# Gate factors held with channels on partitions and applied after y is turned back, with ScalarE sharing the taking out of y

## The chip, the cores and the metric

The kernel runs on one core of one Trainium2 chip. The metric is the time of one execution on the device in microseconds (us); lower is better. The engines of the core are named as in the profile: PE is TensorE, DVE is VectorE, ACT is ScalarE, POOL is GpSimd, SP is SyncE, which issues the transfers.

## The reference

Four layers stand one behind the other, on x of shape (2, 1024, 256). Layers 0 and 3 are attention layers, which the change leaves alone. Layer 1 is a Mamba block and layer 2 a block with two state-space scans, one forward and one backward. Cut to what matters, with 512 channels and 16 states:

```python
# layer 1, both batches
xm, z = split(h @ W_in)                  # 512 channels each
xm = silu(causal_conv(xm) + conv_b)
y = scan(xm) + xm * D_param              # hst = hst * dA + dt*x*B ; y = sum over states of hst * C
out = (y * silu(z)) @ W_out              # z is the gate factor, one for each token and channel

# layer 2, both batches
u1, u2 = two projections of the normed tokens xs
y = scan_forward(u1) + u1 * Dp1 + scan_backward(u2) + u2 * Dp2
out = (y * silu(xs @ Wx.T + bx)) @ Wf.T + bf
```

## The kernel before

Every scan is a *run*: run 0 and run 1 are layer 1 on batch 0 and 1, runs 2 and 3 are the forward and backward scan of layer 2 on batch 0, runs 4 and 5 the same on batch 1. In the code `r.q` is the run's number and `r.n` its kind: 0 for layer 1, 1 for a forward scan of layer 2, 2 for a backward one. A run goes over two halves of 512 tokens (`r.order`, the first is p=0 and the second p=1), and within a half over 16 states and 4 blocks of 128 channels: 128 units, which are handled in 64 pairs. The work of one pair passes through the engines like this:

- PE forms u for each unit into one of the PSUM banks 4 to 7 (`form_u`: L757 or L762), and ACT makes the decay factors (`decay`, L844) and the scaled inputs (L821, L828).
- DVE runs the recurrence along the tokens (L897, one instruction for a unit).
- POOL multiplies a pair with C (L912, one instruction for a pair).
- PE turns the product so that tokens are on partitions and adds it up in PSUM banks 0 to 3 (`add_up`, L781, eight transposes for a pair). Bank j holds y for 128 tokens and all 512 channels.

Between DVE and PE there are five pair buffers (`HS`), so DVE can be at most five pairs ahead of `add_up`. Every engine does its instructions in the order in which the code writes them; engines wait for each other through counters (`wait_ge`).

y is taken out of banks 0 to 3 twice in a run: at unit 71 (`TAKEN_AT`) for the first half, and at the end for the second. DVE does it, one instruction for a bank: in layer 1 it multiplies by silu(z) while taking out (`gated`, L1093), in run 2 and 4 it copies (L1212), in run 3 and 5 it multiplies by the gate factor MX (L1215). Runs 3 and 5 first add what runs 2 and 4 left, through an identity matmul into the same banks (`add_before`, L792).

Behind runs 0, 1, 3 and 5 comes what this text calls the *tail*: `turn_back_t` turns y so that channels are on partitions again, with 32 transposes into eight banks (L920), ACT copies them out (`turn_back_s`, L927), and PE multiplies by W_out or Wf (`tokens_t`, L265). Meanwhile DVE goes on with what stands next in its own order: behind run 1 `norm2_v` for batch 0 and behind run 3 `norm2_v` for batch 1 (two normalisations, one behind the other, L206 to L217, with L973 and L975 between them, and each with one instruction of POOL, L230). Behind run 5 it is `norm3_v` for batch 0 (one normalisation). Then follow the instructions that take the projection out of PSUM: L1101 behind runs 0 and 1, and L1227, L1230, L1232 behind runs 3 and 5. The next layer's first transposes on PE (L243) and its first projection (L256) read what `norm2_v` made.

Ahead of runs 3 and 5, `inputs_t` prepares the run, and `gates_t` computes the gate factors of layer 2 there: for each of eight token tiles a bias matmul (L195) and two matmuls (L1145). ACT applies silu (`gates_s`, L1152). The last four of these have to wait until the last gate is computed, since they overwrite what the gates read (XS):

```python
        XS = area(2048, 2, S)
        MX = area(2048, TB, E)
```

Of the kernel before, what the change touches and what calls it, by code (L numbers as in the profile page):

```python
# [111 lines left out]
def program(nc, T, out):  # L112
    with ExitStack() as ctx:
# [626 lines left out]
        def run_t(e, w, r, before=None):  # L740
# [24 lines left out]
            def open_y(ci, j):  # L765
# [4 lines left out]
                if ci == r.order[0]:  # L770
                    w.wait_ge(*(dve if j < 2 else act).at(("dut", q, 1, j)))
                else:
                    w.wait_ge(*taken.at((q, r.order[0], j)))
# [34 lines left out]
            banks.at, banks.held = 4, [[("last y", q, j)] for j in range(4)] + [[("last u", q, j)] for j in range(4)]  # L808

        def run_s(e, w, r, meanwhile=None):  # L810
# [51 lines left out]
            for i in range(UNITS):  # L862
                k, dt = divmod(i, 4)
                if i >= 4:
                    decay(i)
# [4 lines left out]
                else:  # L870
                    spread_b(i // 8 * 2 + 3, i // 2 % 4)

        TAKEN_AT = 71

        def run_v(e, w, r, take_out):
            q = r.q

            def take_y(ci, pair):
                w.wait_ge(*added.at((q, pair)))
                for j in range(4):  # L880
                    take_out(e, w, 4 * ci + j, PS[:, j, :], (q, ci, j))
# [32 lines left out]
        def turn_back_t(e, w, key, src, ready):  # L914
            for c in range(2):
                for m in range(4):
                    o = take(w, (key, c, m))
                    ready()
                    for j in range(4):
                        t = e.transpose(o[:, j * 128:(j + 1) * 128], src[:, 4 * c + j, m * 128:(m + 1) * 128], ident[:, :])  # L920
                    t.then_inc(*pe.up((key, c, m)))

        def turn_back_s(e, w, key, dst):
            for c in range(2):
# [890 lines left out]
```

## Time and profile before

| what | value |
| --- | --- |
| median of 3 runs | 2087.67 us (2085.17 to 2089.85) |
| time of the profiled execution | 2090.79 us |
| its span in the profile | 2089.0 us |
| busy share: PE, DVE, ACT, POOL | 93%, 76%, 69%, 50% |
| granted clock of PE, mean over the span | 0.969 |

The span is what the profiler saw of the core; the device time of that execution is 1.79 us longer. The busy shares are means over all four layers. POOL stands idle in the first and the last layer and works almost without a break in the six runs, so what bounds a stage must be read from that stage. The granted clock is 1.00 at 2.4 GHz and 0.50 at 1.2 GHz.

### The profile page before, as it was taken

To read this page: it belongs to the slowest core of one execution; us is meant where nothing else is said; L and a number is where in the kernel's file an instruction comes from. 1 tells how busy PE (TensorE), PEld (TensorE's weight loads), DVE (VectorE), ACT (ScalarE), POOL (GpSimd) and SP (SyncE) were. 2 spreads that over 40 slices of the span, in tenths; PEclk is the share of its full clock that TensorE was granted. 3 is DMA by queue.
4 is the path that set the end of the run, shared out by engine and by line. 5 is a ranking of instruction groups with operands and counts; after the bars stand their busy time and mean duration, and the time that the engine had idled before them with its cause. 6 is when DMAs were issued, how large, how long until landed. Compare 5 with 4: busy or idle time off the path is not lost.

```text
span 2089.0 us, 32428 instructions
## 1 busy us (share of the span) xinstructions
PE 1939.5 (93%) x12376; PEld 1356.1 (65%) x12376; DVE 1585.7 (76%) x2084; ACT 1436.9 (69%) x2434; POOL 1035.9 (50%) x598
## 2 busy tenths in 40 slices
PE   6989999899999899989998999899988999999997
PEld 3754999659985799589965998599853222222222
DVE  5556899469984899689974998699859777777632
ACT  3426998389964999598827996898642566655664
POOL 3021799209981599379930997299724000002000
PEclk9989999999999999999999999999999999999999
DMA  5031211111111111011100111111101111111000
GB/s 188 1 129 43 72 56 57 41 39 57 57 41 52 39 58 57 22 36 57 52 10 12 57 57 42 40 53 56 36 16 40 33 33 32 33 33 32 9 21 21
DMA packets 57369, 95.04 MB, mean 45 GB/s; under 512 B 14903, under 2 KB 23383, under 8 KB 55806
## 3 DMA queue, kind: packets, MB, share of 16 engines
q1 hardware_dynamic: 55678, 88.77, 14.1%
q0 software_dynamic: 1536, 4.20, 0.7%
q8 instruction: 98, 1.61, 0.3%
q14 instruction: 57, 0.47, 0.1%
HBM read 73.42 MB, written 6.91 MB: 38 GB/s over the span
## 4 chain that ended last, share of the span: by engine, by line
PE 72%; DVE 10%; issue 6%; POOL 6%; ACT 4%; DMA 1%; SPq 0%; POOLq 0%; DVEq 0%; ACTq 0%
PE PS L757 14%; PE PS L781 12%; PE PS L762 7%; PE PS L256 7%; PE PS L1409 5%; DVE A L1422 5%; PE PS L1457 5%; POOL A L912 5%; PE PS L265 4%; PE PS L1602 3%; PE PS L788 2%; PE PS L1145 1%; PE PS L441 1%; PE PS L644 1%; PE PS L1036 1%
## 5 line engine op out<-in xcount | busy, mean ns | idle before, releaser
L912 POOL TENSOR_TENSOR A<-A 128x1024 f32<-128x1024 f32 x384 | 898.4, 2387 | 333.7 <-ACT small L836 265.9
L844 ACT ACTIVATE A<-A,negA 128x512 f32<-128x512 f32 x768 | 545.0, 712 | 42.5 <-DVE A L897 32.9
L897 DVE TENSOR_TENSOR_SCAN A<-A,PS 128x512 f32<-128x512 f32 x384 | 433.3, 1199 | 52.2 <-PE PS L762 36.0
L897 DVE TENSOR_TENSOR_SCAN A<-A,small,PS 128x512 f32<-128x512 f32 x384 | 455.3, 1257 | 6.0 <-PE PS L757 5.5
L781 PE MATMUL PS<-ident,A 128*128 128x128 f32 x3072 | 401.4, 274 | 16.8 <-POOL A L912 11.6
L1422 DVE TENSOR_REDUCE A<-PS 128x1 f32<-128x512 f32 x512 | 324.9, 682 | 101.5 <-PE PS L1409 99.2
L757 PE MATMUL PS<-A 128*128 128x128 f32 x3072 | 386.5, 277 | 0.1
L1640 ACT ACTIVATE A<-PS 128x1024 f32<-128x1024 f32 x256 | 260.0, 1023 | 183.3 <-PE PS L1602 180.7
L757 PEld LDWEIGHTS PS<-A 128*128 128x128 f32 x3072 | 366.3, 193 | 7.0 <-issue 3.8
L781 PEld LDWEIGHTS PS<-ident,A 128*128 128x128 f32 x3072 | 348.1, 141 | 24.0 <-POOL A L912 14.2
L821 ACT ACTIVATE A<-A,small 128x512 f32<-128x512 f32 x340 | 240.3, 711 | 23.7 <-PE PS L762 23.5
L762 PE MATMUL PS<-ident,A 128*128 128x128 f32 x1360 | 194.8, 280 | 24.9 <-ACT A L821 22.2
L1409 PE MATMUL PS<-A 99*128 99x512 bf16 x480 | 188.6, 398 | 28.2 <-DVE A L1422 14.9
L762 PEld LDWEIGHTS PS<-ident,A 128*128 128x128 f32 x1360 | 160.4, 144 | 34.8 <-issue 27.2
L1387 POOL CAST W<-W 128x32 bf16<-128x32 f32 x32 | 6.7, 209 | 355.3 <-DVE W L1380 341.8
L1602 PE MATMUL PS<-A 102*128 102x512 bf16 x480 | 176.4, 385 | 0.5
L1409 PEld LDWEIGHTS PS<-A 99*128 99x128 bf16 x480 | 46.6, 97 | 165.7 <-DVE A L1422 153.4
L828 ACT ACTIVATE A<-ident,small 128x128 f32<-128x128 f32 x384 | 147.6, 389 | 9.0 <-PE PS L757 9.0
L1457 PE MATMUL PS<-A,W 128*32 128x512 f32 x1024 | 141.5, 605 | 0.0
L1602 PEld LDWEIGHTS PS<-A 102*128 102x128 bf16 x480 | 44.9, 98 | 130.9 <-ACT A L1640 57.6
L230 POOL TENSOR_TENSOR RS<-VE,HALF 128x8 f32<-128x8 f32 x14 | 23.1, 1649 | 211.5 <-DVE VE L225 211.4
L256 PE MATMUL PS<-A,W 128*128 128x512 f32 (+1 forms) x288 | 126.6, 597 | 0.7 <-ACT A L250 0.7
(192 smaller groups left out, 1939.8 us busy)
## 6 DMA issues: line engine op xcount, KB each, us to landing
A<-scrc SPq DMA_DIRECT2D x192, 256.0 KB, 3.1
A<-A SPq DMA_DIRECT2D x360, 32.0 KB
scr<-A SPq DMA_DIRECT2D x4, 1024.0 KB, 4.8
W<-in_wa SPq DMA_DIRECT2D x2, 1536.0 KB, 9.6
X<-in_x SPq DMA_DIRECT2D x4, 512.0 KB, 5.5
scr<-W SPq DMA_DIRECT2D x128, 1.5 KB
out<-X SPq DMA_DIRECT2D x2, 1024.0 KB, 4.4
W<-in_w SPq DMA_DIRECT2D x1, 1984.0 KB, 7.2
```

The source lines that it names most:

```text
L256: t = e.matmul(o[0:M, :], wt(k, m), act_in(k), start=k == 0, stop=k == nk - 1)
L757: t = e.matmul(o[:, j * 128:(j + 1) * 128], r.DUT[:, 4 * ci + j, dt * 128:(dt + 1) * 128], DB[k // 2 % 2][:, j, :], start=True, stop=True)
L762: t = e.transpose(o[:, j * 128:(j + 1) * 128], r.G[(2 * k + j) % 6][:, dt * 128:(dt + 1) * 128], ident[:, :])
L781: t = e.matmul(PS[:, j, dt * 128:(dt + 1) * 128], r.H[pair % HS][:, dt % 2, j * 128:(j + 1) * 128], ident[:, :], start=open_y(ci, j), stop ...
L844: e.activation(A_B[i % 4], r.DT[:, dt, ci * 512:(ci + 1) * 512], ACT.Exp, scale=negA[:, r.n, dt * 16 + s:dt * 16 + s + 1]).then_inc(*decay ...
L897: e.tensor_tensor_scan(h, a, u, init, ALU.mult, ALU.add).then_inc(*scanned.up((q, i)))
L912: e.tensor_tensor(h, h, CB[k % 2].unsqueeze(1).broadcast_to([128, 2, 512]), ALU.mult).then_inc(*weighed.up((q, pair)))
L1409: e.matmul(o, SQ[j][0:99, nt * 128:(nt + 1) * 128], SK3[j][0:99, c * 512:(c + 1) * 512], start=True, stop=True).then_inc(*pe.up(("trial", ...
L1422: e.tensor_reduce(NM[:, k % 2, q:q + 1], bank(("trial", k, nt, c)), AX.X, ALU.max, negate=True).then_inc(*dve.up(("trial", k, nt, c)))
L1457: t = e.matmul(PV[32 * j:32 * j + 32, c, :], V[:, tile * 272 + 17 * h:tile * 272 + 17 * h + 32], PX[mt % 2][j][:, c * 512:(c + 1) * 512], ...
L1602: t = e.matmul(PS[:, banks.place[key] + c, :], SK3[sl][0:102, mt * 128:(mt + 1) * 128], SQ[sl][0:102, c * 512:(c + 1) * 512], start=True, ...
L1640: e.activation(PX[mt % 2][j], PS[:, i:i + 2, :].rearrange("p a b -> p (a b)"), ACT.Exp).then_inc(*act.up(("weights", u, mt, j)))
```

## The change

The gate factors of both layers are made with channels on partitions (ZT for layer 1, MX for layer 2). In layer 2 the bias moves from a matmul into the ACT instruction that applies silu. y is taken out without a gate: in runs 0, 1, 2 and 4 ACT takes all four banks at the middle of the run and banks 2 and 3 at its end, and DVE takes banks 0 and 1 at the end. In runs 3 and 5 DVE takes all of them, and adds the forward scan's y in the same instruction; the identity matmuls `add_before` are gone. The first half is turned back between the last two `add_up`, and the second half behind the last; both go out of PSUM through a DVE multiplication with the gate factors (`turn_back_v`), where ACT copied before. The projection behind the tail waits for each half apart, and in layer 2 it begins with the half that was done first.

```diff
+        def took(r, p, j):
+            return act.at(("took", r.q, p, j)) if by_scalar(r, p, j) else taken.at((r.q, p, j))
+        def by_scalar(r, p, j):
+            return r.n < 2 and (p == 0 or j >= 2)
+        def take_s(e, w, r, p, j, y):
+            w.wait_ge(*added.at((r.q, PAIRS_N // 2 * (p + 1) - 1)))
+            e.activation(y(4 * r.order[p] + j), PS[:, j, :], ACT.Copy).then_inc(*act.up(("took", r.q, p, j)))
+        def take_v(e, w, r, p, j, y):
+            o = y(4 * r.order[p] + j)
+            w.wait_ge(*added.at((r.q, PAIRS_N // 2 * (p + 1) - 1)))
+            if r.n == 2:
+                e.tensor_tensor(o, o, PS[:, j, :], ALU.add).then_inc(*taken.up((r.q, p, j)))
+            else:
+                e.tensor_copy(o, PS[:, j, :]).then_inc(*taken.up((r.q, p, j)))
...
-            def add_before(ci, j):
-                e.matmul(PS[:, j, :], ident[:, :], before[:, 4 * ci + j, :], start=open_y(ci, j), stop=True, skip_group_check=True)
...
-                if dt == 3 and 8 <= s < 12 and before is not None:
-                    add_before(ci, s - 8)
...
             for pair in range(PAIRS_N - 3, PAIRS_N):
+                if pair == PAIRS_N - 1 and back:
+                    back(0)
                 add_up(pair)
+            if back:
+                back(1)
...
             for i in range(UNITS):
                 k, dt = divmod(i, 4)
+                if i == TAKEN_AT + 1:
+                    for j in range(4):
+                        if by_scalar(r, 0, j):
+                            take_s(e, w, r, 0, j, y)
                 if i >= 4:
                     decay(i)
...
+            for j in range(4):
+                if by_scalar(r, 1, j):
+                    take_s(e, w, r, 1, j, y)
...
-            take_y(r.order[1], PAIRS_N - 1)
+            if back:
+                back(0)
+            take_y(1)
+            if back:
+                back(1)
...
+        def turn_back_t(e, w, r, p, y):
+            c = r.order[p]
+            for m in range(4):
+                o = take(w, ("back", r.q, p, m))
+                for j in range(4):
+                    w.wait_ge(*took(r, p, j))
+                    t = e.transpose(o[:, j * 128:(j + 1) * 128], y(4 * c + j)[:, m * 128:(m + 1) * 128], ident[:, :])
+                t.then_inc(*pe.up(("back", r.q, p, m)))
+        def turn_back_v(e, w, r, p, dst, gates):
+            o = slice(r.order[p] * 512, (r.order[p] + 1) * 512)
+            for m in range(4):
+                w.wait_ge(*pe.at(("back", r.q, p, m)))
+                e.tensor_tensor(dst[:, m, o], bank(("back", r.q, p, m)), gates[:, m, o], ALU.mult).then_inc(*dve.up(("back", r.q, p, m)))
...
                 for j in range(0, TB, 2):
-                    w.wait_ge(*act.at((("yt", b), 1, 3)))
+                    w.wait_ge(*dve.at(("back", b, j // 4, 3)))
...
         def gates_t(e, w, b):
-            for i in GATES:
-                o = take(w, ("mx", b, i))
-                bias_t(e, o, "l2bx")
-                for k in range(2):
-                    t = e.matmul(o, XS[:, k, i * 128:(i + 1) * 128], Wx[:, k, :], start=False, stop=k == 1)
-                t.then_inc(*pe.up(("mx", b, i)))
+            for m, c in GATES:
+                project_t(e, w, ("mx", b, m, c), lambda k, m: Wx[:, k, m * 128:(m + 1) * 128], 2, m, lambda k: XS[:, k, c * 512:(c + 1) * 512])
...
-                for j in range(0, TB, 2):
-                    w.wait_ge(*act.at((("yt2", b), 1, 3)))
+                for j in (4, 6, 0, 2):
+                    w.wait_ge(*dve.at(("back", 3 + 2 * b, 0 if j >= 4 else 1, 3)))
```

The first place is PE at the end of run 1. L781 is `add_up` (L800 in the changed kernel), L920 the transposes that turn y back (L951), L265 the projection, L243 the transposes that open layer 2. Before:

```order
L757 MATMUL PS<-A 128x128 x8
L781 MATMUL PS<-ident,A 128x128 x40
L920 MATMUL PS<-ident,A 128x128 x32
L265 MATMUL PS<-W,A 128x256 x32
L243 MATMUL PS<-ident,A 128x128 x16
```

And with the change:

```order
L776 MATMUL PS<-A 128x128 x8
L800 MATMUL PS<-ident,A 128x128 x32
L951 MATMUL PS<-ident,A 128x128 x16
L800 MATMUL PS<-ident,A 128x128 x8
L951 MATMUL PS<-ident,A 128x128 x16
L265 MATMUL PS<-W,A 128x256 x32
L243 MATMUL PS<-ident,A 128x128 x16
```

Half of the transposes has moved ahead of the last eight of `add_up`; the others stand where they stood.

The second place is DVE at the end of run 1. L897 is the recurrence (L922 in the changed kernel), L1093 the gated taking out, L206 to L975 belong to `norm2_v`. Before:

```order
L897 SCALAR_TENSOR_TENSOR A<-A,small,PS 128x512 x7
L1093 TENSOR_TENSOR A<-PS,A 128x512 x4
L897 SCALAR_TENSOR_TENSOR A<-A,small,PS 128x512 x57
L1093 TENSOR_TENSOR A<-PS,A 128x512 x4
L206 BN_STATS ST<-X 128x6 x8
```

And with the change, where L757 is the plain copy out of PSUM (`take_v`) and L958 the multiplication by the gate factors (`turn_back_v`):

```order
L922 SCALAR_TENSOR_TENSOR A<-A,small,PS 128x512 x64
L958 TENSOR_TENSOR A<-PS,A 128x512 x4
L757 COPY A<-PS 128x512 x2
L958 TENSOR_TENSOR A<-PS,A 128x512 x4
L206 BN_STATS ST<-X 128x6 x8
```

Ten instructions stand between the last unit of the recurrence and `norm2_v`, where four stood; the four at unit 71 are gone from DVE.

The third place is PE ahead of run 3, where the gate factors of layer 2 are made. L644 and L648 belong to `inputs_t`, L659 are the run's own transposes. Before (the pair of rows L195 and L1145 comes eight times):

```order
L644 MATMUL PS<-A,W 128x512 x8
L648 MATMUL PS<-ident,A 128x96 x8
L195 MATMUL PS<-ROW,ones 128x512
L1145 MATMUL PS<-W,A 128x512 x2
```

And with the change:

```order
L644 MATMUL PS<-A,W 128x512 x8
L648 MATMUL PS<-ident,A 128x96 x8
L256 MATMUL PS<-A,W 128x512 x16
L659 MATMUL PS<-ident,A 128x128 x32
```

The eight bias matmuls are gone, and the sixteen others now stand in one row.

## Rows read from the trace of the kernel before

**Rows 1.** The page: the chain that ended last, share of the span by engine.

```profile
PE 72%; DVE 10%; issue 6%; POOL 6%; ACT 4%; DMA 1%; SPq 0%; POOLq 0%; DVEq 0%; ACTq 0%
```

**Rows 2.** Timeline of POOL, runs 2 and 3: start, duration, instructions, idle before.

```profile
701.26 119.33 POOL L912 TENSOR_TENSOR A<-A 128x1024 f32<-128x1024 f32 x51 [43.42 <-ACT small L836]
820.87 30.47 POOL L912 TENSOR_TENSOR A<-A 128x1024 f32<-128x1024 f32 x13 [0.27 <-DVE A L897]
...
902.06 46.87 POOL L912 TENSOR_TENSOR A<-A 128x1024 f32<-128x1024 f32 x20 [50.72 <-ACT small L836]
...
1036.12 9.66 POOL L912 TENSOR_TENSOR A<-A 128x1024 f32<-128x1024 f32 x4 [0.89 <-DVE A L897]
1046.06 11.72 POOL L912 TENSOR_TENSOR A<-A 128x1024 f32<-128x1024 f32 x5 [0.28 <-DVE A L897]
```

**Rows 3.** Windows in runs 2 and 3: busy time by engine, PE clock.

```profile
770.00:853.00 83.00, 80.05 (x704) 77.65 (x703) 78.86 (x70) 66.00 (x118) 80.92 (x35) 1.00 0.17 52
900.00:975.00 75.00, 74.98 (x647) 72.70 (x646) 70.99 (x64) 70.56 (x157) 70.69 (x31) 0.99 0.17 50
```

**Rows 4.** Timeline of all engines ahead of run 3.

```profile
852.32 7.03 PE L256 MATMUL PS<-A,W 128*96 128x512 f32 x16
...
867.15 0.38 PE L195 MATMUL PS<-ROW,ones 3*128 3x512 bf16 x1
...
880.30 2.29 DVE L713 TENSOR_TENSOR A<-A 128x2048 f32<-128x2048 f32 x1
...
882.77 0.38 PE L195 MATMUL PS<-ROW,ones 3*128 3x512 bf16 x1
...
885.11 2.06 ACT L1152 ACTIVATE A<-PS 128x512 f32<-128x512 f32 x4 [6.59 <-PE PS L1145]
```

**Rows 5.** Timeline of all engines in the tail of run 0.

```profile
367.64 1.09 PE L781 MATMUL PS<-ident,A 128*128 128x128 f32 x8 [0.69 <-POOL A L912]
...
369.97 1.09 PE L781 MATMUL PS<-ident,A 128*128 128x128 f32 x8 [1.24 <-POOL A L912]
371.10 2.48 DVE L1093 TENSOR_TENSOR A<-PS,A 128x512 f32<-128x512 f32 x4 [3.61 <-PE PS L781]
...
373.73 6.65 PE L920 MATMUL PS<-ident,A 128*128 128x128 f32 x32 [2.67 <-DVE A L1093]
...
381.11 14.08 PE L265 MATMUL PS<-W,A 128*128 128x256 f32 x64 [0.73 <-ACT A L927]
```

**Rows 6.** Timeline of DVE, then PE, in the tail of run 1.

```profile
617.26 2.48 DVE L1093 TENSOR_TENSOR A<-PS,A 128x512 f32<-128x512 f32 x4 [3.61 <-PE PS L781]
...
637.47 2.67 DVE L217 TENSOR_SCALAR A<-W,MV,RS 128x256 f32<-128x256 f32 x8 [1.75 <-POOL RS L230]
...
641.00 1.91 PE L243 MATMUL PS<-ident,A 128*128 128x128 f32 x16
643.14 20.87 PE L256 MATMUL PS<-A,W 128*128 128x512 f32 x48 [0.23 <-ACT A L250]
```

**Rows 7.** Timeline of DVE, then PE, in the tail of run 3.

```profile
1079.17 2.67 DVE L217 TENSOR_SCALAR A<-A,MV,RS 128x256 f32<-128x256 f32 x8 [1.75 <-POOL RS L230]
...
1084.79 1.91 PE L243 MATMUL PS<-ident,A 128*128 128x128 f32 x16
```

**Rows 8.** Timeline of DVE in the tail of run 5.

```profile
1510.53 2.67 DVE L217 TENSOR_SCALAR A<-X,MV,RS 128x256 f32<-128x256 f32 x8 [1.75 <-POOL RS L230]
...
1530.34 0.69 DVE L1232 TENSOR_TENSOR X<-X,A 128x512 f32<-128x512 f32 x1
```

**Rows 9.** Windows, tail of run 3; then a PE row of layer 3.

```profile
1063.00:1064.00 1.00, 1.00 (x7) 1.00 (x6) 1.00 (x5) 0.76 (x2) 0.00 (x0) 0.50 0.00 0
...
1066.00:1067.00 1.00, 0.94 (x9) 0.70 (x7) 0.40 (x2) 0.90 (x2) 0.56 (x1) 1.00 0.00 0
...
1536.76 15.67 PE L1302 MATMUL PS<-A,W 128*128 128x512 f32 x32 [3.54 <-ACT A L250]
```

**Rows 10.** Timeline of DVE in the middle of run 0.

```profile
297.29 2.46 DVE L1093 TENSOR_TENSOR A<-PS,A 128x512 f32<-128x512 f32 x4
```

More of the change, by code:

```diff
@@ L772, in open_y @@
                 else:
-                    w.wait_ge(*taken.at((q, r.order[0], j)))
+                    w.wait_ge(*took(r, 0, j))
                 return True
@@ L803, in run_t, with run_s @@
                     add_skip(ci, s - 4)
[L804 to L805 removed]
+            banks.at, banks.held = 4, [[("last y", q, j)] for j in range(4)] + [[("last u", q, j)] for j in range(4)]
             for pair in range(PAIRS_N - 3, PAIRS_N):
+                if pair == PAIRS_N - 1 and back:
+                    back(0)
                 add_up(pair)
[L808 to L810 removed]
+            if back:
+                back(1)
+        def run_s(e, w, r, y, meanwhile=None):
             q = r.q
@@ L897, in run_v @@
                 e.tensor_tensor_scan(h, a, u, init, ALU.mult, ALU.add).then_inc(*scanned.up((q, i)))
-            take_y(r.order[1], PAIRS_N - 1)
+            if back:
[3 more added lines that the diff above has]
+                back(1)
             for j in range(4):
-                banks.give(("last y", q, j), taken.at((q, r.order[1], j)))
+                banks.give(("last y", q, j), took(r, 1, j))
                 banks.give(("last u", q, j), scanned.at((q, UNITS - 4 + j)))
@@ L912, in run_p @@
                 e.tensor_tensor(h, h, CB[k % 2].unsqueeze(1).broadcast_to([128, 2, 512]), ALU.mult).then_inc(*weighed.up((q, pair)))
[L914 to L924, printed above, removed]
-                for m in range(4):
-                    w.wait_ge(*pe.at((key, c, m)))
-                    e.activation(dst[:, m, c * 512:(c + 1) * 512], bank((key, c, m)), ACT.Copy).then_inc(*act.up((key, c, m)))
-                    banks.give((key, c, m), act.now())
+        def turn_back_t(e, w, r, p, y):
[11 more added lines that the diff above has]
+                e.tensor_tensor(dst[:, m, o], bank(("back", r.q, p, m)), gates[:, m, o], ALU.mult).then_inc(*dve.up(("back", r.q, p, m)))
+                banks.give(("back", r.q, p, m), dve.now())
         Wzs = W2[:, 3968:4992].rearrange("p (k n) -> p k n", k=4)
@@ L1115, in program, with y2 @@
         XS = area(2048, 2, S)
-        GATES = (4, 5, 6, 7, 0, 1, 2, 3)
+        GATES = [(m, c) for m in (2, 3, 0, 1) for c in range(2)]
+        def y2(i):
+            return YT2[:, i, :]
         def norm3_v(e, w, b):
@@ L1140, in gates_t @@
         def gates_t(e, w, b):
-            for i in GATES:
-                o = take(w, ("mx", b, i))
-                bias_t(e, o, "l2bx")
-                for k in range(2):
-                    t = e.matmul(o, XS[:, k, i * 128:(i + 1) * 128], Wx[:, k, :], start=False, stop=k == 1)
-                t.then_inc(*pe.up(("mx", b, i)))
+            for m, c in GATES:
+                project_t(e, w, ("mx", b, m, c), lambda k, m: Wx[:, k, m * 128:(m + 1) * 128], 2, m, lambda k: XS[:, k, c * 512:(c + 1) * 512])
         def gates_s(e, w, b):
-            for i in GATES:
-                w.wait_ge(*pe.at(("mx", b, i if i >= 4 else 3)))
-                e.activation(MX[:, i, :], bank(("mx", b, i)), ACT.Silu).then_inc(*act.up(("mx", b)))
-                banks.give(("mx", b, i), act.now())
+            for m, c in GATES:
+                w.wait_ge(*pe.at(("mx", b, m, c) if m >= 2 else ("mx", b, 1, 1)))
+                e.activation(MX[:, m, c * 512:(c + 1) * 512], bank(("mx", b, m, c)), ACT.Silu, bias=col("l2bx", m)).then_inc(*act.up(("mx", b)))
+                banks.give(("mx", b, m, c), act.now())
         def layer2_sp(e, w):
@@ L1223, in layer2_v @@
                     norm3_v(e, w, 0)
-                for j in range(0, TB, 2):
+                for j in (4, 6, 0, 2):
                     v, x = SK[:, j:j + 2, :], X[:, b * TB + j:b * TB + j + 2, :]
```

68 lines of the change are left out of this document (31 added, 37 removed).

## Prediction

> **What bounds the kernel now.** I read the page's chain first [rows 1]. It gives PE 72% and POOL 6%, but it is a sum over stages, and inside a run the engines keep step so closely that it can name any of them. So I went to POOL's timeline. In run 2 it works from 701.26 to 851.34 (820.87 + 30.47), 150.1 us for 64 pairs or 2.345 us each, with one gap of 0.27 us [rows 2]. A run of this kind has the length of POOL's work, and what is saved on DVE, PE or ACT inside it is worth nothing. Run 3 is another case: 902.06 to 1057.78 is 155.7 us, 5.6 more for the same 64 multiplications, with gaps that end on DVE. The windows show why. Their columns are the window, its length, the busy times of PE, PEld, DVE, ACT and POOL, and the granted clock. In the first half of run 3 PE is busy 74.98 of 75 us; in the second half of run 2 it is 80.05 of 83 and ACT 66.00 of 83 [rows 3]. PE is what holds run 3 up.
>
> Between the runs the engines work one behind the other. Ahead of run 3 eight gates follow each other on PE at (882.77 - 867.15)/7 = 2.23 us, and ACT's silu at 885.11 waits for the last [rows 4]. In the tail of run 0 everything waits in turn: last `add_up` at 369.97, DVE 371.10 to 373.58, 32 transposes 373.73 to 380.38, projection from 381.11 [rows 5].
>
> **The run's interior.** In runs 3 and 5 `add_before` goes. With that PE has in run 3 just what it has in run 2, so I give both runs run 2's length: 155.7 - 150.1 = 5.6 us each, **-11.2**. It can't be more, since POOL's work is the floor.
>
> In the middle of runs 0, 1, 2 and 4 the taking out moves from DVE (four in 2.46 us [rows 10]) to ACT. POOL never stopped there, so the gain is 0. The danger is on ACT: its four copies wait for `add_up` of pair 31, and behind them stand `decay` of unit 72 and all later ones, on which DVE waits. From the end of that `add_up` I count four copies at about 0.5 us (four ACT outputs from PSUM take 2.06 [rows 4]), a decay of 0.7 and, on DVE, two units of 1.25, in all some 5.4 us until pair 36 is ready. DVE stands four pairs ahead of POOL, 9.4 us less what `add_up` itself takes (1.09 [rows 5]). The cover holds with about 3 us, and DVE's own 2.46 us, which fell in the same place, are gone. I take 0; without cover it would be at most 5.4 us in each of four runs.
>
> **Gates.** Ahead of runs 3 and 5, 8 bias matmuls and their changes of type go. Sixteen rows of the plain form take 7.03 us [rows 4], so 32 take 14.1 where 8 x 2.23 = 17.8 stood: 3.8 us each, **-7.6**. The other branch leaves room: the second DVE product ends at 882.59 (880.30 + 2.29), and PE needs it only for its second sixteen transposes, at about 883.7 then. The layer 1 gates only swap operands, 0.
>
> **The tails**, all counted from the end of POOL's last multiplication. `turn_back_t` of the first half (16 transposes at 0.11 us, the rate of `add_up`, 1.8 us in all) begins at 367.64 + 1.09 = 368.73 in run 0. POOL ends at 369.92, so the last `add_up` starts some 0.5 us late and ends at about 371.6. DVE is free of its first four multiplications (2.48 us, as its taking out [rows 5]) at 371.8.
>
> - *Run 0.* DVE and ACT take two banks each, ready by 373.0. The 16 remaining transposes last until 375.0 at the full clock. The projection needs only the first half, done long ago, and starts at 375.1 instead of 381.11: -6.0. If the clock falls, as it does in the tails now (32 transposes in 6.65 us are 0.21 each), transposes and projection lose about 3, and -3.0 is left. PE now idles about 1 us where it idled 2.67, so I take **-6.0**.
> - *Run 1.* The same gain on PE, but PE isn't the last. `norm2_v` ends on DVE at 640.14 and PE's L243 starts at 641.00, reading its last tile [rows 6]: DVE is 0.9 us ahead of PE. DVE used to be free for it at 619.74. Now the two takings follow on `add_up`, then a wait for the transposes and four multiplications, which end at about 622.1 (full clock) or 622.8 (half): `norm2_v` is 2.4 to 3.1 us later and ends at about 642.6. PE, ready at 635, waits. Eight of L243 stand behind the last tile, so L256 starts at about 643.8 instead of 643.14, +0.6, and it starts after some 5 us with little work. In layer 3 a row behind 3.54 us of idleness took 15.67 us for 32 [rows 9] where two times 7.03 would be 14.1 or less, 1.6 to 1.9 more; I take 2.0. Together **+2.6**, with 0.2 (no clock loss) and 4.2 as its ends. The tail's whole gain is lost and a little more.
> - *Run 3.* DVE takes all four banks here, so its path is longer: free 3.5 to 4.2 us later than now. `norm2_v` ended at 1081.84, 2.95 before L243 [rows 7]; now it ends at 1085.3 to 1086.0, and PE, ready at about 1081.5, waits again. L256 starts about where it did (-0.9 to +0.3), with a clock loss of 0 to 2.0. I take **+0.9**, ends -0.9 and +2.3.
> - *Run 5.* Behind it stands only one normalisation, which ended at 1513.20, and the end is the last L1232 at 1531.03 [rows 8], bound by the projection. The projection starts 4.1 us earlier at the full clock. PE idles about 2.5 us here while DVE takes four banks, near the 2.67 behind which the clock was low, and at half clock only 1.3 is left. I take **-3.0**.
> - *Runs 2 and 4.* PE goes straight on into `inputs_t` and ACT's two copies fit in its idle time: 0.
>
> On the clock the trace shows this: at 1063 it is 0.50 (1.2 GHz), at 1066 it is 1.00, and between them PE ran nothing but L920 transposes [rows 9]. So transposes alone brought it back.
>
> The Trainium skill, "TensorE: Matmul & The Clock Gate", Part 4, says otherwise: transposes in PE's transpose mode don't count as work for the clock, which doesn't rise for them. The trace disagrees at this place. By that rule all four tails would take the half-clock ends named above.
>
> **Sum.** -11.2 - 7.6 - 6.0 + 2.6 + 0.9 - 3.0 = **-24.3 us**. The profiled execution took 2090.8, so 2066.5 for a like one; it stands 3.1 above the median of the runs shown, so on the median 2087.67 - 24.3 = **2063.4**.
>
> **Rivals.**
> - *`norm2_v` has room after all* (8%). If DVE isn't last behind runs 1 and 3, they give -6.0 and -4.1 instead of +2.6 and +0.9: -37.9, 2050. For it speaks run 3's 2.95 us of room, against it run 1's 0.86 and ten DVE instructions where four stood.
> - *Half clock in all tails* (8%). -3.0, +4.2, +2.3 and -1.3 in place of my values is 7.7 less gain: -16.6, 2071. For it speaks that every tail now has a stretch at 0.50, against it the shorter idle time and [rows 9].
> - *`add_before` isn't what stretches runs 3 and 5* (6%), but say the backward order of the recurrence: -13.1, 2075. Against it stands PE at 74.98 of 75 us.
> - *The gates are hidden* (5%), the next step then waiting for DVE's product or ACT's table load: -16.7, 2071.
> - *Slower* (2%). ACT's copies in the middle of runs 0, 1, 2 and 4 use up DVE's lead and ACT never regains it, so that ACT paces the second halves. Those are 128 pairs; it decides at 24.3/128 = 0.19 us a pair, that is 2.53 instead of 2.345. At 2.60 a pair it would be +33 - 24, 2096. ACT's 66.00 of 83 us speaks against it.
> - *No effect* (3%): POOL's pace is the whole story in runs 3 and 5 too, and the tails' gains are eaten by DVE everywhere, within 4 us of 2087.7.
>
> The forecast keeps 68%, with its own range of 2058 to 2069. The range from 2056 to 2071.5 leaves out the first and third rival, the last two and the edges. A measurement of this kernel tells about 0.2%, some 4 us, from no change. Faster by more than that: 0.95, within: 0.03, slower: 0.02.
>
> **What the profile after would show.** POOL from first to last multiplication in about 150.2 us in all six runs. Gates ahead of run 3: 16 rows (32 instructions) without bias in 14 us. In the tail of run 0 the projection about 5.2 us behind POOL's end, where 11.2 stood. In the tail of run 1 a gap on PE of 5 us ahead of L243, released by DVE, and L256 at a clock of 0.50 at first. I am wrong if that gap isn't there, if POOL waits for ACT's decays in the middle of runs 0, 1, 2 or 4, or if run 3 keeps its 155 us.

## Result and the profile after

The changed kernel took 2059.82 us (median of 4 runs, 2057.59 to 2062.47) against 2086.42 for the kernel before on the same chip (4 runs, 2085.02 to 2089.85): a ratio of 0.9871, 95% interval 0.9853 to 0.9888. Measured again, five runs on another chip gave 2059.39 (2051.31 to 2061.58) against 2088.57, a ratio of 0.9853 (0.9836 to 0.9869). The prediction was 2063.4, range 2056 to 2071.5. One execution of a later kernel (experiment 8, measured again) took 2458.91 us at a mean granted clock of 0.741, where the others had 0.971 to 0.975, and is left out below.

The profiled execution took 2062.47 with a span of 2060.7. Against the 2090.8 of the profile before that is -28.3 us. The page of the changed kernel first: busy time, share of the span and instructions of each engine, and the chain that ended last.

```profile
PE 1916.8 (93%) x12328; PEld 1344.4 (65%) x12328; DVE 1587.8 (77%) x2092; ACT 1426.2 (69%) x2426; POOL 1035.1 (50%) x598
PE 56%; POOL 15%; DVE 12%; issue 11%; ACT 4%; DMA 1%; SPq 0%; POOLq 0%; DVEq 0%; ACTq 0%
```

POOL's share of the chain went from 6% to 15% [rows 1]. Most of that lies in runs 0, 1, 2 and 4. Here is the timeline of POOL (start, duration, instructions, idle before): the first row is run 2, the others are run 3.

```profile
693.51 149.27 POOL L941 TENSOR_TENSOR A<-A 128x1024 f32<-128x1024 f32 x64 [41.67 <-ACT small L854]
...
889.66 37.38 POOL L941 TENSOR_TENSOR A<-A 128x1024 f32<-128x1024 f32 x16 [46.88 <-ACT small L854]
927.23 81.92 POOL L941 TENSOR_TENSOR A<-A 128x1024 f32<-128x1024 f32 x35 [0.18 <-DVE A L922]
1009.43 30.49 POOL L941 TENSOR_TENSOR A<-A 128x1024 f32<-128x1024 f32 x13 [0.28 <-DVE A L922]
```

Run 3 lasts from 889.66 to 1039.92, 150.3 us where 155.7 stood [rows 2]. Run 2 has become a single unbroken row of 149.27 where there were two rows and 150.1. Run 3 still has small gaps that end on DVE; experiment 3 shows what they mean.

These rows cut the whole kernel into thirteen pieces: the six runs, each from the start of POOL's first multiplication to the end of its last, and what lies between, ahead and behind. All pieces of all kernels below come from such rows. (The column "again" is the profile of the changed kernel measured again, experiment 9.)

| piece | before | changed | again | changed - before | forecast |
|---|---|---|---|---|---|
| ahead of run 0 | 219.75 | 219.40 | 219.85 | -0.35 | 0 |
| run 0 | 150.17 | 149.31 | 149.33 | -0.86 | 0 |
| tail of run 0 to run 1 | 95.84 | 89.27 | 87.75 | -6.57 | -6.0 |
| run 1 | 150.31 | 149.48 | 149.06 | -0.83 | 0 |
| tail of run 1 to run 2 | 85.19 | 86.05 | 87.10 | +0.86 | +2.6 |
| run 2 | 150.08 | 149.28 | 149.20 | -0.80 | 0 |
| gates, to run 3 | 50.72 | 46.87 | 47.00 | -3.85 | -3.8 |
| run 3 | 155.72 | 150.26 | 150.13 | -5.46 | -5.6 |
| tail of run 3 to run 4 | 87.27 | 87.64 | 87.50 | +0.37 | +0.9 |
| run 4 | 150.26 | 149.25 | 149.26 | -1.01 | 0 |
| gates, to run 5 | 50.72 | 48.66 | 47.01 | -2.06 | -3.8 |
| run 5 | 155.72 | 150.13 | 150.11 | -5.59 | -5.6 |
| tail of run 5, layer 3 | 587.25 | 585.10 | 584.90 | -2.15 | -3.0 |
| sum | | | | -28.3 | -24.3 |

PE in the tail of run 0 of the changed kernel, from the timeline:

```profile
367.38 1.91 PE L951 MATMUL PS<-ident,A 128*128 128x128 f32 x16
369.12 1.04 PE L800 MATMUL PS<-ident,A 128*128 128x128 f32 x8
371.15 0.33 PE L951 MATMUL PS<-ident,A 128*128 128x128 f32 x1 [0.99 <-DVE A L757]
371.75 1.86 PE L951 MATMUL PS<-ident,A 128*128 128x128 f32 x15 [0.27 <-DVE A L757]
373.44 4.91 PE L265 MATMUL PS<-W,A 128*128 128x256 f32 x22
```

Sixteen transposes lie ahead of the last `add_up` (L800). The other sixteen take 0.33 and 1.86 us, where all 32 took 6.65 in one row behind it [rows 5], and the projection (L265) starts at 373.44, 4.73 behind POOL's end at 368.71. Before it was 11.2.

The tail of run 1, timeline of DVE and then of PE:

```profile
611.08 2.48 DVE L958 TENSOR_TENSOR A<-PS,A 128x512 f32<-128x512 f32 x4 [0.64 <-PE PS L951]
613.67 2.71 DVE L206 BATCH_NORM_STATS2 ST<-X 128x6 f32<-128x256 f32 x8
...
631.48 2.67 DVE L217 TENSOR_SCALAR A<-W,MV,RS 128x256 f32<-128x256 f32 x8 [1.75 <-POOL RS L230]
...
612.19 13.98 PE L265 MATMUL PS<-W,A 128*128 128x256 f32 x64
631.95 3.71 PE L243 MATMUL PS<-ident,A 128*128 128x128 f32 x16 [5.79 <-DVE A L217]
635.50 20.77 PE L256 MATMUL PS<-A,W 128*128 128x512 f32 x48
```

PE ends the projection at 626.2 and then waits 5.79 us for L217, the end of `norm2_v`. This wait took the place of the one removed, as forecast: from POOL's end on, PE is 6.4 us earlier than before (18.7 for 25.1 at the projection's end) and DVE 2.6 later (26.7 for 24.1 at the end of `norm2_v`).

### The profile page after: what moved, and what is told of

Same layout as the page of the kernel before. It is cut to its first block, busy times and chain, and to the rows that moved or that the text cites. A ratio compares the mean times of both kernels' runs of the same rounds, so it can differ in the third digit from the quotient of the medians.

```text
span 2060.7 us, 32328 instructions
## 1 busy us (share of the span) xinstructions
PE 1916.8 (93%) x12328; PEld 1344.4 (65%) x12328; DVE 1587.8 (77%) x2092; ACT 1426.2 (69%) x2426; POOL 1035.1 (50%) x598
## 4 chain that ended last, share of the span: by engine, by line
PE 56%; POOL 15%; DVE 12%; issue 11%; ACT 4%; DMA 1%; SPq 0%; POOLq 0%; DVEq 0%; ACTq 0%
POOL A L941 14%; PE PS L256 9%; PE PS L776 8%; PE PS L800 7%; PE PS L1431 5%; DVE A L1444 5%; PE PS L1479 5%; PE PS L781 4%; PE PS L1624 3%; PE PS L265 2%; PE PS L441 1%; PE PS L644 1%; PE PS L807 1%; PE PS L1324 1%; DVE A L922 1%
## 5 line engine op out<-in xcount | busy, mean ns | idle before, releaser
L922 DVE TENSOR_TENSOR_SCAN A<-A,PS 128x512 f32<-128x512 f32 x384 | 431.2, 1198 | 47.6 <-PE PS L781 36.0
L922 DVE TENSOR_TENSOR_SCAN A<-A,small,PS 128x512 f32<-128x512 f32 x384 | 453.8, 1261 | 8.3 <-ACT A L862 5.2
L800 PE MATMUL PS<-ident,A 128*128 128x128 f32 x3072 | 402.5, 274 | 11.8 <-POOL A L941 8.4
L800 PEld LDWEIGHTS PS<-ident,A 128*128 128x128 f32 x3072 | 349.0, 142 | 18.2 <-POOL A L941 10.5
L781 PE MATMUL PS<-ident,A 128*128 128x128 f32 x1360 | 193.3, 280 | 25.6 <-ACT A L839 22.3
L256 PE MATMUL PS<-A,W 128*128 128x512 f32 (+1 forms) x416 | 182.9, 598 | 0.4 <-ACT A L250 0.2
L781 PEld LDWEIGHTS PS<-ident,A 128*128 128x128 f32 x1360 | 159.8, 144 | 31.2 <-issue 23.1
L256 PEld LDWEIGHTS PS<-A,W 128*128 128x128 f32 (+1 forms) x416 | 76.2, 186 | 99.9 <-issue 93.1
```

Source lines behind the costliest of these rows:

```text
L256: t = e.matmul(o[0:M, :], wt(k, m), act_in(k), start=k == 0, stop=k == nk - 1)
L781: t = e.transpose(o[:, j * 128:(j + 1) * 128], r.G[(2 * k + j) % 6][:, dt * 128:(dt + 1) * 128], ident[:, :])
L800: t = e.matmul(PS[:, j, dt * 128:(dt + 1) * 128], r.H[pair % HS][:, dt % 2, j * 128:(j + 1) * 128], ident[:, :], start=open_y(ci, j), stop ...
L922: e.tensor_tensor_scan(h, a, u, init, ALU.mult, ALU.add).then_inc(*scanned.up((q, i)))
```

## Experiments

The edits below are to the changed kernel. A time is a median, and a ratio compares it with the kernel before on the same chip: 2089.79 us for experiments 1 to 4, 2087.03 for 5 to 8, 2088.57 for 9. The changed kernel itself has the ratios 0.9871 and 0.9853, so experiments are compared with it by their ratios, and by the pieces of the profiles. One and the same kernel differs by about 1.5 us in a tail from profile to profile (the changed kernel's two profiles in the table: 89.27 and 87.75, 86.05 and 87.10).

**1. The identity matmuls back in runs 3 and 5** (`e1_add_before`). The forward scan's y is again added into PSUM by PE, and DVE copies plainly.

```diff
+            def add_before(ci, j):
+                e.matmul(PS[:, j, :], ident[:, :], before[:, 4 * ci + j, :], start=open_y(ci, j), stop=True, skip_group_check=True)
...
+                if dt == 3 and 8 <= s < 12 and before is not None:
+                    add_before(ci, s - 8)
```

> The changed kernel with one part undone: in runs 3 and 5 the forward scan's y is added again by identity matmuls inside the run, and DVE takes y out by plain copies. Theory A, that these matmuls stretch runs 3 and 5 because PE has no room there: POOL's stretch from first to last multiplication grows from 150.26 and 150.13 us to about 155.7 in both, everything else stays, and the whole kernel is about 11 us slower than the changed one, near 2071. Rival, that the stretch came from the gated taking out or from the backward order of the recurrence: both runs stay at about 150.2 and the time at 2060.

It took 2075.72 us (2068.44 to 2075.91), ratio 0.9933 (0.9907 to 0.9958). By the ratio that is 13 us slower than the changed kernel, where 11 were expected. Runs 3 and 5 are back at 155.76 and 155.75 us; the other four stay at 149.3 to 149.7. From the timeline of POOL in run 3:

```profile
890.93 46.90 POOL L946 TENSOR_TENSOR A<-A 128x1024 f32<-128x1024 f32 x20 [46.99 <-ACT small L859]
938.91 9.47 POOL L946 TENSOR_TENSOR A<-A 128x1024 f32<-128x1024 f32 x4 [1.08 <-DVE A L927]
949.44 25.73 POOL L946 TENSOR_TENSOR A<-A 128x1024 f32<-128x1024 f32 x11 [1.06 <-DVE A L927]
```

The first row is that of before [rows 2], and gaps follow it again. DVE is named as the releaser, but nothing was added on DVE: the identity matmuls were put back on PE, and DVE's addition became a copy. These matmuls own the 5.5 to 5.6 us of each run.

**2. A bias matmul back ahead of each gate** (`e2_bias_matmul`). The bias is so added twice; ACT still adds it too.

```diff
+                o = take(w, ("mx", b, m, c))
+                bias_t(e, o, "l2bx")
+                for k in range(2):
+                    t = e.matmul(o, Wx[:, k, m * 128:(m + 1) * 128], XS[:, k, c * 512:(c + 1) * 512], start=False, stop=k == 1)
```

> The changed kernel with the bias matmul back ahead of each gate (the bias is all zeros in this data, so the result is the same). Theory B, that the gates' row of matmuls on PE is what sets the end of this stage: the stretch between POOL's last multiplication of run 2 and its first of run 3 goes from 46.88 us back to about 50.7, the same ahead of run 5, in all 7.6 us slower than the changed kernel, near 2067.5. Rival, that swapping the operands or the ACT bias gave the gain: within 2 us of the changed kernel.

It took 2071.36 (2069.09 to 2072.7), ratio 0.992 (0.9901 to 0.994), by the ratio 10 us slower than the changed kernel, where 7.6 were expected. The pieces ahead of runs 3 and 5 are 52.79 and 50.94, where the changed kernel has 47.0 undisturbed: 3.9 us for the second. The first holds a fall of the clock besides, L256 taking 8.32 us for the 7.03 of [rows 4]. Here is PE ahead of run 3, first in this kernel and below it in the changed one:

```profile
844.21 8.32 PE L256 MATMUL PS<-A,W 128*96 128x512 f32 x16
...
860.34 0.38 PE L195 MATMUL PS<-ROW,ones 3*128 3x512 bf16 x1
860.65 1.98 PE L1177 MATMUL PS<-A,W 128*128 128x512 f32 x4
862.57 0.38 PE L195 MATMUL PS<-ROW,ones 3*128 3x512 bf16 x1
```

```profile
858.51 13.93 PE L256 MATMUL PS<-A,W 128*128 128x512 f32 x32
873.30 4.05 PE L659 MATMUL PS<-ident,A 128*128 128x128 f32 x32 [0.87 <-ACT A L1180]
```

Eight pairs at a pitch of 2.23 us (17.8 in all) against one row of 13.93: that is the whole gain. The wait for ACT behind it is 0.87 us in both.

**3. Taking out at the middle by DVE** (`e3_middle_by_dve`).

```diff
-            return r.n < 2 and (p == 0 or j >= 2)
+            return r.n < 2 and p == 1 and j >= 2
```

> The changed kernel with DVE instead of ACT taking y out in the middle of runs 0, 1, 2 and 4. In the changed kernel POOL's stretch in these runs is 149.3 to 149.5 us, where it was 150.1 to 150.3 before. Theory C, that DVE's 2.46 us in the middle use up its lead over POOL, so that from about pair 51 on DVE paces the run: the four runs go back to 150.1 to 150.3 with POOL's gap of 0.27 us near pair 51 back, in all 3.5 us slower. Rival, my prediction's own reading, that DVE's cover is complete and the difference has another cause (C's transfers, ACT): the four runs stay below 149.6.

It took 2063.31 (2062.88 to 2065.25), ratio 0.9887 (0.9868 to 0.9905). The median alone doesn't tell it from the changed kernel, but the pieces do: runs 0, 1, 2 and 4 are back at 150.20, 150.32, 150.07 and 150.08. POOL in run 2 has the two rows of before again, which the changed kernel doesn't have:

```profile
693.27 119.35 POOL L941 TENSOR_TENSOR A<-A 128x1024 f32<-128x1024 f32 x51 [42.71 <-ACT small L854]
812.88 30.46 POOL L941 TENSOR_TENSOR A<-A 128x1024 f32<-128x1024 f32 x13 [0.26 <-DVE A L922]
```

So moving four instructions of 2.46 us from DVE [rows 10] is worth 0.8 to 0.9 us in each of four runs. I had costed it at nothing. DVE's own rows in the middle of run 2 show why, first of the kernel before (L897 is the recurrence), then of the changed one, where ACT takes y out (L749):

```profile
761.61 8.97 DVE L897 TENSOR_TENSOR_SCAN A<-A,PS 128x512 f32<-128x512 f32 x8
...
778.70 2.46 DVE L1212 COPY A<-PS 128x512 f32<-128x512 f32 x4
781.08 28.21 DVE L897 TENSOR_TENSOR_SCAN A<-A,small,PS 128x512 f32<-128x512 f32 x24
```

```profile
762.75 9.46 DVE L922 TENSOR_TENSOR_SCAN A<-A,small,PS 128x512 f32<-128x512 f32 x8
770.80 2.06 ACT L749 ACTIVATE A<-PS 128x512 f32<-128x512 f32 x4 [2.06 <-PE PS L800]
773.50 27.11 DVE L922 TENSOR_TENSOR_SCAN A<-A,small,PS 128x512 f32<-128x512 f32 x23 [1.29 <-ACT A L862]
```

In the first half a pair costs DVE 2 x 8.97/8 = 2.24 us, less than POOL's 149.27/64 = 2.332, so its lead over POOL grows. In the second half it costs 2 x 28.21/24 = 2.35, a little more than POOL's, so a lead that is spent there doesn't come back. And the lead is small. In the changed kernel DVE has finished pair 35 (counted from 0) at 762.75 + 9.46 = 772.2, and POOL comes to it at 693.51 + 35 x 2.332 = 775.1: 2.9 us. The kernel before spent 2.46 of that on the taking out. The difference in pace and two waits of DVE for PE (0.25 and 0.21 us, in both kernels) used up the rest by pair 51, where POOL's row breaks [rows 2], and from then on POOL went at DVE's pace, 30.47/13 = 2.344 us a pair. In the changed kernel DVE waits 1.29 us for ACT at that place, and the remainder lasts to the end of the run. Runs 3 and 5 of the changed kernel, where DVE still takes y out in the middle, have the same rows at the end (30.49 and 30.48 for 13 pairs) and last 150.1 to 150.3. Whether the same move would gain as much there was not tried.

**4. `norm2_v`'s first statistics ahead of runs 1 and 3** (`e4_early_statistics`). They read X, which is there long before. DVE computes them and POOL their powers ahead of the run; behind it only the rest of `norm2_v` stands. `add_first` moves ahead of `inputs_v`.

```diff
                 run_p(e, w, runs[2 + 2 * b])
+                if b == 0:
+                    norm_p(e, w, ("ln2a", 1), range(TB))
...
                     if n:
+                        if b == 0:
+                            norm2_early_v(e, w, 1)
                         inputs_v(e, w, runs[3 + 2 * b])
```

> The changed kernel with the statistics of norm2's first normalisation (DVE 3.5 us and POOL's power, 1.7) moved out of the tails of runs 1 and 3 to where DVE is idle, ahead of runs 1 and 3. Theory D, that behind runs 1 and 3 DVE's chain is last: norm2 ends about 5.4 us earlier; run 1's stretch from POOL's last multiplication to its next first goes from 86.06 to about 80 us (norm2 then ends near the end of the projection, so the clock loss shrinks too), run 3's from 87.64 to about 84, where the projection becomes last; the whole about 9 us faster than the changed kernel, near 2051. Rival, that what is lost there is the clock alone or that PE is last: less than 2 us faster.

It took 2047.51 (2043.97 to 2052.01), ratio 0.9816 (0.979 to 0.9842), faster than both kernels. The tails of runs 1 and 3 fell from 86.05 and 87.64 to 80.10 and 82.62, where about 80 and 84 were expected. Timeline of DVE, then PE, behind run 1:

```profile
604.90 2.48 DVE L958 TENSOR_TENSOR A<-PS,A 128x512 f32<-128x512 f32 x4 [0.64 <-PE PS L951]
607.30 2.67 DVE L1009 TENSOR_SCALAR W<-X,MV,RS 128x256 f32<-128x256 f32 x8
...
606.01 13.98 PE L265 MATMUL PS<-W,A 128*128 128x256 f32 x64
620.33 3.03 PE L243 MATMUL PS<-ident,A 128*128 128x128 f32 x16 [0.34 <-DVE A L217]
```

The wait of 5.79 us is down to 0.34. The same rows of `norm2_v` decide when L243 can start, so DVE paced this tail, and the PE time that the change had saved there comes out once DVE's path is shorter.

**5. Both halves turned back behind the last `add_up`** (`e5_turn_back_behind`).

```diff
-                if pair == PAIRS_N - 1 and back:
-                    back(0)
                 add_up(pair)
             if back:
+                back(0)
                 back(1)
```

> The changed kernel with the first half turned back behind the last add_up instead of ahead of it, and DVE's takings ahead of both multiplications. Theory E, from the rows of the changed kernel: the 16 transposes of the first half then run on PE while the second half is taken out, a time in which PE is idle anyway, so placing them ahead of the last add_up is worth little to PE; what moves is DVE's order. The projection of run 0 starts about 5.1 us behind POOL's end where it is 4.7, DVE is free for norm2 1.3 us later behind run 1 and 1.6 behind run 3, and the whole is 3 to 4 us slower than the changed kernel. Rival, that the early transposes save their own 1.8 us in each of four tails: projections 1.8 us later, the whole 7 us slower.

It took 2061.25 (2057.76 to 2065.88), ratio 0.9886 (0.9868 to 0.9905), not told apart from the changed kernel, where 3 to 4 us slower was expected. In the tail of run 0:

```profile
364.61 1.09 PE L800 MATMUL PS<-ident,A 128*128 128x128 f32 x8 [1.21 <-POOL A L939]
365.54 3.66 PE L949 MATMUL PS<-ident,A 128*128 128x128 f32 x32
369.47 8.90 PE L265 MATMUL PS<-W,A 128*128 128x256 f32 x40 [0.28 <-DVE A L956]
```

L949 is `turn_back_t` here. The projection starts 4.9 us behind POOL's end (364.55), hardly later than in the changed kernel (4.73): the first half's transposes now run while the second half is taken out, a time in which PE waited 0.99 us anyway. Behind run 1 the piece is 88.58, 2.5 more than in the profile of the changed kernel and 1.5 more than in its second one. DVE's first four products now follow on the copies, and `norm2_v` begins 7.35 us behind POOL's end where it was 6.22: that accounts for 1.1. The rest is about what L256 took longer, 22.07 us for 20.77 and 21.58 in the two profiles of the changed kernel.

**6. The projection waits for both halves** (`e6_wait_for_both`).

```diff
-                    w.wait_ge(*dve.at(("back", b, j // 4, 3)))
+                    w.wait_ge(*dve.at(("back", b, 1, 3)))
...
-                    w.wait_ge(*dve.at(("back", 3 + 2 * b, 0 if j >= 4 else 1, 3)))
+                    w.wait_ge(*dve.at(("back", 3 + 2 * b, 1, 3)))
```

> The changed kernel with the projection behind the tail waiting for both halves. Theory: it starts when DVE's last multiplication ends, 1.4 us later behind run 0 (6.15 instead of 4.73 us behind POOL's end) and 1.3 later behind run 5; behind runs 1 and 3 DVE's norm2 is last, so nothing is lost there; in all 2.7 us slower. Rival, that PE is last behind all four: 5 us slower. If the wait for the halves apart were what gave the whole tail's gain, run 0's stretch to the next run would go from 89.3 back to near 95.

It took 2060.96 (2057.5 to 2066.13), ratio 0.9886 (0.9865 to 0.9906), where 2.7 us slower than the changed kernel was expected. In the tail of run 0 the wait is there:

```profile
367.45 1.86 PE L951 MATMUL PS<-ident,A 128*128 128x128 f32 x15 [0.27 <-DVE A L757]
...
370.57 5.66 PE L265 MATMUL PS<-W,A 128*128 128x256 f32 x25 [1.26 <-DVE A L958]
```

That is 1.26 us, and the piece is 90.92 for 89.27 and 87.75 in the two profiles of the changed kernel. Behind runs 1 and 3, where DVE paces the tail, the pieces are 86.63 and 87.34, no longer than the changed kernel's. Behind run 5 the last piece is 584.49, no longer either, though 1.3 more was expected. The median doesn't show the difference.

**7. DVE takes all four banks at the end** (`e7_no_sharing_at_end`).

```diff
-            return r.n < 2 and (p == 0 or j >= 2)
+            return r.n < 2 and p == 0
```

> The changed kernel with DVE taking all four banks at the end of runs 0, 1, 2 and 4 (ACT still takes them in the middle). Theory: the second half is turned back about 1.1 us later behind run 0, as it is behind run 3, so run 0's stretch to the next run goes from 89.3 to about 90.4; behind run 1 norm2 is about 1.1 us later, 86.05 to about 87.2; behind runs 2 and 4 nothing; in all 2.2 us slower. Rival, that the sharing at the end gives nothing since ACT and DVE then wait for the same add_up: no change.

It took 2063.39 (2062.81 to 2063.84), ratio 0.9888 (0.9872 to 0.9905), not told apart from the changed kernel by the median. The tails of runs 0 and 1 are 91.81 and 87.34, where about 90.4 and 87.2 were expected. PE in the tail of run 0, and two windows there (window, length, busy time of PE, PEld, DVE, ACT and POOL, granted clock, DMA share and GB/s):

```profile
373.51 3.04 PE L951 MATMUL PS<-ident,A 128*128 128x128 f32 x13 [0.27 <-DVE A L757]
...
373.00:375.00 2.00, 1.73 (x8) 1.54 (x9) 1.27 (x3) 0.00 (x0) 0.00 (x0) 0.57 0.00 0
375.00:377.00 2.00, 2.00 (x11) 1.92 (x10) 1.68 (x3) 0.00 (x0) 0.00 (x0) 0.58 0.00 0
```

The four copies take 2.47 us for 1.28, and the last transposes start 1.2 us later. The clock fell there too: 13 transposes in 3.04 us, where the 15 of the changed kernel took 1.86.

That can be counted over all profiles. Where DVE and ACT share the banks, the 15 transposes behind them took 1.85 or 1.86 us in each of 20 tails (ten profiles, runs 0 and 1; this experiment and experiment 5, whose transposes stand in one row, aside). Where DVE takes all four, the 13 took 1.64 us in 14 tails and 2.08 to 3.04 in 10 of 24 (runs 3 and 5 of the same profiles, all four tails of this experiment). So the longer stretch, in which PE stands idle 0.27 us three times, goes with a fall of the clock in four cases of ten, and the shorter one, with one such idle time, never in these profiles. The two tails that this experiment changed are one of each: 3.04 us behind run 0, 1.64 behind run 1.

**8. Experiment 4 with five unused products where PE idles between layers 2 and 3** (`e8_keep_busy`).

```diff
+            w.wait_ge(*dve.at(("back", 5, 1, 3)))
+            w.wait_ge(*transfer("w3").at(0))
+            keep_busy(e, 0, 2)
             layer2_done(w)
             turned_norm_t(e, w, 0)
-            w.wait_ge(*transfer("w3").at(0))
+            keep_busy(e, 7, 3)
```

> The kernel with the early statistics, and in addition five matmuls that compute nothing needed, put into PE's idle time between layer 2 and layer 3 (two ahead of L243, three behind it, 128x512 in f32 each). Theory F, that the 32 instructions of layer 3's first projection take 15.7 to 17 us instead of 14 because PE's clock falls in the 2.4 and 3.0 us of idleness ahead of them: they take 14 here with the clock at 1.00, the stretch from POOL's last multiplication of run 5 to the end is 2 to 3.5 us shorter than the 585.15 us of the kernel with the early statistics. Rival, that idleness isn't what lowers the clock, or that the extra matmuls delay L243 themselves: 585 or more.

It took 2047.42 (2043.54 to 2052.79), ratio 0.9814 (0.979 to 0.9839). First the changed kernel's PE at the start of layer 3 and two windows, then this kernel's PE (L1611 are the unused products, two records each):

```profile
1500.94 2.46 PE L243 MATMUL PS<-ident,A 128*128 128x128 f32 x16 [2.43 <-DVE X L1254]
1506.42 16.96 PE L1324 MATMUL PS<-A,W 128*128 128x512 f32 x32 [3.01 <-ACT A L250]
...
1503.00:1512.00 9.00, 5.99 (x9) 2.52 (x9) 7.03 (x26) 3.47 (x5) 3.28 (x2) 0.50 0.01 3
1512.00:1515.00 3.00, 3.00 (x7) 1.15 (x7) 1.91 (x7) 1.85 (x3) 0.00 (x0) 0.93 0.00 0
```

```profile
1491.67 2.74 PE L1611 MATMUL PS<-W,ident 128*128 128x512 f32 x6
1495.28 14.00 PE L1339 MATMUL PS<-A,W 128*128 128x512 f32 x32 [0.86 <-ACT A L250]
```

The same 32 matmuls take 14.00 us and not 16.96, and the last piece is 581.55 where experiment 4 has 585.15. Locally the theory holds. But the medians of experiments 4 and 8 are 0.1 us apart (on different chips).

**9. Repetitions**, five rounds each on one chip: the changed kernel, experiment 4 and experiment 8, unchanged.

> The changed kernel once more, in more rounds, on the chip on which the next two run. Its time should be within 0.15% of 2059.8.

> The kernel with the early statistics once more. Theory D holds if it is again 9 to 13 us faster than the changed kernel on the same chip; if the first difference came from where PE's clock happened to fall, it is less than 5 us.

> The kernel with the early statistics and the extra matmuls once more. Theory F: 2 to 3.6 us faster than the one without them, as the profile of its last stage said (581.55 instead of 585.15 us from POOL's last multiplication of run 5 to the end). Rival, from the equal medians of the first time: no difference in the whole, since the clock falls elsewhere instead.

| kernel | median us | range | ratio (interval) |
|---|---|---|---|
| changed | 2059.39 | 2051.31 to 2061.58 | 0.9853 (0.9836 to 0.9869) |
| experiment 4 | 2048.85 | 2047.39 to 2052.74 | 0.9817 (0.9805 to 0.983) |
| experiment 8 | 2048.71 | 2047.7 to 2050.4 | 0.9812 (0.98 to 0.9825) |

Experiment 4 is 10.5 us faster than the changed kernel on the same chip; the tails of runs 1 and 3 are 80.09 and 84.29 there, against 87.09 and 87.50. Experiment 8 has 581.66 in the last piece for 582.57: this time experiment 4 lost less there by itself, and the filling matmuls have gained nothing that the median shows. That is the rival named ahead of the run, not its theory.

## Why the prediction was right, point by point

- *Runs 3 and 5* (-11.2): -11.05. Experiment 1 gives it back, so `add_before` was the stretch. The floor was not quite POOL's work, which is 149.3 us: at the end of these runs DVE still sets the pace (experiment 3).
- *The middle by ACT* (0): -3.5 over four runs. This is the term that was mis-sized. The step that failed is "POOL never stopped there, so the gain is 0". I took the 0.27 us gap in [rows 2] for nothing, and the run's 150.1 us for POOL's own pace. Experiment 3 shows that DVE's 2.46 us used up its lead over POOL, so that DVE paced the end of the run. Behind it stands a wrong reading of the lead: "DVE stands four pairs ahead of POOL", where the rows give 2.9 us, little more than one pair. As a sum for ACT's cover the working holds, since the 9.4 us are what POOL takes for pairs 32 to 35, and POOL indeed doesn't wait in run 2. But the cover was 1.5 us and not 3: pair 36 was ready about 5 us behind `add_up` of pair 31, as counted, and that `add_up` ended (770.8, where ACT's copies begin) 2.5 us behind POOL's multiplication and not 1.09.
- *Gates* (-3.8 each): -3.85 and -2.06, and -3.72 and -3.71 in the second profile. The 2.06 holds a fall of the clock at the end of run 4, where the last eight of `add_up` took 1.94 us for 1.09 and sixteen instructions of L256 took 7.90 us for 7.03.
- *Tail of run 0* (-6.0): -6.57, and -8.09 again. The projection starts 4.73 us behind POOL's end, forecast about 5.2. Read off the rows, the 6.5 us by which it starts earlier are these: PE's idle time for the taking out fell from 2.67 to 0.99 (1.7), the transposes behind it from 6.65 to about 2.3, since half of them lie ahead and the clock stayed full (4.4), and the wait of 0.73 in front of the projection is gone, against 0.3 for the later `add_up`. Experiments 5 to 7 undo single steps: where the first half's transposes stand is worth nothing that can be told here, the separate wait 1.3 us, ACT's sharing 1.2. The full clock was not tried by itself; the same 32 transposes take 3.66 us in experiment 5, 3.0 less than 6.65.
- *Tail of run 1* (+2.6): +0.86, and +1.91 again. The step was right: PE waits 5.79 us for `norm2_v`, and experiment 4 removes the wait and 6 us with it. L256 starts 28.05 behind POOL's end where it was 27.07, so +1.0 for the forecast +0.6. The clock term, 2.0, was mis-sized: it measured 0 in this profile and 0.8 in the second. The windows of the changed kernel show why.

```profile
630.00:632.00 2.00, 0.05 (x1) 0.05 (x1) 0.52 (x2) 0.00 (x0) 1.45 (x1) 0.50 0.00 0
632.00:634.00 2.00, 2.00 (x8) 1.57 (x9) 2.00 (x7) 0.56 (x1) 0.00 (x0) 0.50 0.00 0
634.00:635.00 1.00, 1.00 (x7) 1.00 (x6) 1.00 (x3) 0.93 (x2) 0.00 (x0) 0.50 0.00 0
635.00:636.00 1.00, 1.00 (x7) 0.76 (x6) 1.00 (x3) 0.92 (x3) 0.00 (x0) 0.89 0.00 0
```

  The clock was at 0.50 (1.2 GHz) while PE ran the L243 transposes. They took 3.71 us for 1.91, but their last eight had to wait for L217's end at 634.15 in any case, and L256 began 1.35 us behind that, where I had counted 1.2. The clock was back at full then, and L256 took 20.77 us for 20.87 [rows 6]. In the second profile it came back only 1.6 us after L256 had begun, which took 21.58. So "L256 at a clock of 0.50 at first" came in one of two profiles, and cost less than half of what I took.
- *Tail of run 3* (+0.9): +0.37. L256 starts 0.54 earlier against POOL's end than before, inside my -0.9 to +0.3. What follows was not in my working: L256's first groups wait for banks of the projection that DVE frees behind `norm2_v`, three instructions of 0.7 us for each. ACT takes their outputs 2.0 us apart, where it was 1.7 before, and L256 lasts 21.78 us for 20.87.
- *Tail of run 5* (-3.0): -2.15. The projection ended 4.2 us earlier at the full clock, and layer 3 gave back 2.0, since L1324 took 16.96 us behind an idle time of 3.01, where 15.67 stood [rows 9] and 14.00 is possible (experiment 8), and the L243 row ahead of it 2.46 for 1.94.
- *The rivals.* "`norm2_v` has room" fell with the 5.79 us wait. "Half clock in all tails" fell in runs 0 and 1 (15 transposes in 1.86 us) and 5 (13 in 1.64); behind run 3 the clock did fall among them (13 in 2.41), and behind run 1 only later, in the wait for `norm2_v`. The Trainium skill, "TensorE: Matmul & The Clock Gate", Part 4, says that transposes don't bring the clock back. The windows above are a second place that disagrees: between 632 and 635.5 PE ran nothing but L243 transposes, and the clock rose from 0.50 to full. "`add_before` isn't what stretches" fell with experiment 1, "gates are hidden" with experiment 2, "slower" with POOL's single row, and "no effect" with the time.

The sum was 4.0 us short (-24.3 for -28.3). The middle makes 3.5 of it, the tails of runs 0, 1 and 3 make 2.8, and the second gates and the tail of run 5 give 2.6 back; the rest are pieces of less than 0.4. That the total came so close is partly luck: errors of 6.3 us one way and 2.6 the other partly cancel.

## What to carry to other kernels

When a stage is unbroken except for one small gap, measure the pace on both sides of the gap: a lead that is used up late looks like "this engine is the floor" and is not. Read the lead from the two engines' rows and not from the number of buffers between them: five pair buffers lie between DVE and `add_up` here, and DVE's lead over POOL was 2.9 us, little more than one pair. When a wait between two stages is removed on one engine, compute at once when the other inputs of the next stage are ready, and shorten that path with the same change: here the statistics of `norm2_v` could be made before the run, and that was worth 10.5 us more. Work on PE that is moved out of the way of a wait (the transposes ahead of the last `add_up`) need not be worth anything if PE would otherwise do it while it waits for another engine, as it does in experiment 5.

## What the runs showed of the hardware

PE's clock falls in different places in different executions of like code. The piece ahead of run 0 took 219.40 in the changed kernel and 215.30 in experiment 4, where the granted clock averaged 0.92 over the first 220 us of the one and 0.95 over the first 216 of the other. Experiment 4 moves nothing into this stretch, and measured again it took 217.03; over all profiles of the changed kernel and its variants it lies between 215.10 and 219.98. The falls read above cost 0.4 us (13 transposes in 2.08 for 1.64) to 3.0 us (L1324 in 16.96 for 14.00) each, and one kernel's own times spread by up to 10 us (2051.31 to 2061.58), so a local gain of 3.6 us (experiment 8) can be true in a profile and absent from the median.

A POOL multiplication of 128x1024 has a pitch of 2.332 us when nothing makes it wait and 2.344 when it keeps step with DVE; that difference of 0.5% shows in no gap. A unit of DVE's recurrence costs about 1.12 us in the first half of a run, where its start value is a constant (8.97 for 8), and 1.175 in the second, where it is read from a tile (28.21 for 24).
